# Block numbers for TensorE: 32 loaded at the head of a turn instead of 16 at every second group, in all passes of a graph network kernel

## The reference

```python
# block 0, per layer: weighted mean of the neighbours
msg = h[src] * edge_weight[:, None]
h = h @ W_self.T + segment_sum(msg, dst) * inv_deg @ W_neigh.T + b
# block 1: attributes of the edges
m = (h * norm_out)[src] * (a_mu + exp(a_ls) * edge_attr)
h = segment_sum(m, dst) * norm_in @ W + b
# block 2 (GATv2, 5 heads): attention over pairs
e = leaky_relu(xl[src] + xr[dst]); alpha = einsum(e, att)
out = segment_sum(softmax_by_dst(alpha) * xl[src], dst)
# block 3 (RGAT, 8 relations, 4 heads): scores by edge type
alpha = leaky_relu(q[etype, dst] + k[etype, src])
out = segment_sum(softmax_by_dst(alpha) * xw[etype, src], dst)
```

## Time and profile before

| what | value |
|---|---|
| time, median of 3 runs | 9910.92 us (9910.38 to 9911.04) |
| span of the profiled execution | 11974.2 us |
| TensorE matmul busy | 7534.2 us (63%), weight loads 5244.5 us (44%) |
| VectorE busy | 7367.7 us (62%) |
| GpSimd busy | 5383.2 us (45%) |
| ScalarE busy | 2310.3 us (19%) |
| mean granted TensorE clock | 0.733 |

### The profile page before, as it was taken

One profiled execution on the slowest core, in us unless ns is written; L12 is line 12 of the kernel. 1 busy time (PEld: TensorE's weight loads), 2 busy tenths in 40 slices (PEclk: granted clock), 3 DMA queues, 4 the chain that ended last, 5 costly groups with the idle time before them and its releaser, 6 DMA issues. The chain is left out here.

```text
span 11974.2 us, 162471 instructions
## 1 busy us (share of the span) xinstructions
PE 7534.2 (63%) x38295; PEld 5244.5 (44%) x38296; DVE 7367.7 (62%) x10447; ACT 2310.3 (19%) x8712; POOL 5383.2 (45%) x5649
## 2 busy tenths in 40 slices
PE   2878788667677775555548555554855554855557
PEld 1666566555555552333347323333732222622226
DVE  6665433355555555677799567778955555745558
ACT  0222344300000001111159111114910000000000
POOL 2555555455545543665400266550015553055550
PEclk9888888788878885777755577775557666867768
DMA  2333344344444444766649566664933333333333
GB/s 60 87 84 84 99 114 114 90 113 111 110 95 113 111 96 163 234 233 231 194 203 411 179 232 232 229 216 173 415 120 74 74 73 63 116 72 75 75 72 100
DMA packets 851293, 1717.47 MB, mean 143 GB/s; under 512 B 384638, under 2 KB 473541, under 8 KB 796922
## 3 DMA queue, kind: packets, MB, share of 16 engines
q1 hardware_dynamic: 465500, 1137.96, 27.5%
q0 software_dynamic: 207456, 413.40, 15.8%
q10 hardware_dynamic: 178256, 165.14, 4.1%
HBM read 1263.59 MB, written 453.99 MB: 143 GB/s over the span
## 5 line engine op out<-in xcount | busy, mean ns | idle before, releaser
L556 POOL DMA_INDIRECT gathered_rows<-node_table,index x2496 | 2379.1, 953 | 2000.0 <-issue 652.4
L719 PE MATMUL ps_G<-table_parts,low_onehots 125*128 125x320 bf16 x15600 | 2712.0, 336 | 294.1 <-issue 220.8
L576 PE MATMUL ps_sum<-messages,onehots 128*125 128x65 f32 (+3 forms) x13312 | 2113.4, 321 | 993.1 <-issue 643.6
L576 PEld LDWEIGHTS ps_sum<-messages,onehots 128*125 128x125 f32 x13312 | 2011.7, 236 | 1117.9 <-issue 1111.2
L556 POOL DMA_INDIRECT gathered_rows<-xl_table,index x1664 | 1576.7, 948 | 1828.5 <-issue 1028.0
L556 POOL DMA_INDIRECT gathered_rows<-rel_table,index x1456 | 1391.9, 956 | 2009.8 <-ACT index L546 1020.9
L1524 PE MATMUL ps_Z<-xr,onehots_wide 125*128 x3328 | 1505.3, 610 | 1194.5 <-issue 628.4
L719 PEld LDWEIGHTS ps_G<-table_parts,low_onehots 125*128 125x128 bf16 x15600 | 1677.7, 110 | 1183.2 <-issue 312.8
L749 DVE TENSOR_TENSOR rows_by_feature<-ps_G,fifth_onehots 128x320 f32<-128x320 f32 x1040 | 507.0, 487 | 2271.9 <-remote 1683.0
L1524 PEld LDWEIGHTS ps_Z<-xr,onehots_wide 125*128 125x128 f32 x3328 | 801.4, 257 | 1899.3 <-issue 1802.7
L1572 DVE TENSOR_TENSOR z<-gathered_rows,ps_Z 128x650 f32<-128x650 f32 x832 | 670.9, 828 | 835.4 <-issue 499.7
(11 more groups left out here) (326 smaller groups left out, 7209.2 us busy)
## 6 DMA issues: line engine op xcount, KB each, us to landing
stash_a<-gathered_rows SPq DMA_DIRECT2D x208, 1300.0 KB
kept_rows<-stash_a SPq DMA_DIRECT2D x208, 1300.0 KB
onehots<-onehots_kept SPq DMA_DIRECT2D x520, 500.0 KB
onehots_turned<-onehots_turned SPq DMA_DIRECT2D x416, 250.0 KB
stash_r<-gathered_rows ACTq DMA_DIRECT2D x208, 272.0 KB
kept_rows<-stash_r SPq DMA_DIRECT2D x208, 272.0 KB
low_rows<-low_rows SPq DMA_DIRECT2D x416, 125.0 KB
onehots_kept<-onehots ACTq DMA_DIRECT2D x104, 500.0 KB
```

The costliest lines, as they stand in the source:

```text
L556: pool.indirect_dma_start(G[:, HALF * k + q, 0:width], None, table, bass.IndirectOffsetOnAxis(IDX[:, k, q:q + 1], 0)).then_inc(gathered[k] ...
L576: return nc.tensor.matmul(ps_sum[0:BN, bass.ds(at, width)], S[:, j, :], M, start=False, stop=True, skip_group_check=True)
L719: last = nc.tensor.matmul(ps_G[:, (fetch * k + g) % 2, 0:D * FIVE], OT[0:BN, k, g, a, :], HP[:, part, a, :, :].rearrange("p f b -> p (f b) ...
```

## The change

In all six places the load is made at group 0 alone, for all 32 chunks of the turn, and the indexing loses its `% PAIR`. The number of block numbers loaded per turn stays 32, the number of load instructions goes from two to one per turn. The three forms of the edit:

```diff
-                                if k % 2 == 0:
-                                    at = blocks_of(i * U + HALF * k, PAIR)
+                                if k == 0:
+                                    at = blocks_of(i * U, U)
...
-                                    last = sum_chunk(ps_sum, S, j, M[:, j, :], D, at[j % PAIR] * D)
+                                    last = sum_chunk(ps_sum, S, j, M[:, j, :], D, at[j] * D)
```

```diff
-                                if m % 8 == 0:
-                                    at = blocks_of(i * U + 2 * m, PAIR)
+                                if m == 0:
+                                    at = blocks_of(i * U, U)
```

```diff
-                                    if q == 0 and h % 2 == 0:
-                                        at = blocks_of(HALF * (HT * i + h), PAIR)
+                                    if q == 0 and h == 0:
+                                        at = blocks_of(HALF * HT * i, HALF * HT)
```

More of the change, by code:

```diff
@@ L35 @@
 GROUPS = NCH // HALF
-PAIR = 2 * HALF
 NG = NS // HALF
@@ L903, in turn @@
                                 n = K * i + k
-                                if k % 2 == 0:
-                                    at = blocks_of(i * U + HALF * k, PAIR, places[0:1, :], (NB - 1) * (D + 1) + (NB - 1) // PER * (BANK - PER * (D + 1)))
+                                if k == 0:
+                                    at = blocks_of(i * U, U, places[0:1, :], (NB - 1) * (D + 1) + (NB - 1) // PER * (BANK - PER * (D + 1)))
                                 if not hist:
@@ L922, in turn @@
                                 for j in range(HALF * k, HALF * (k + 1)):
-                                    last = sum_chunk(ps_sum, S, j, M[:, j, :], D + 1, at[j % PAIR])
+                                    last = sum_chunk(ps_sum, S, j, M[:, j, :], D + 1, at[j])
                                 last.then_inc(chunk_done.sem, HALF)
@@ L1524, in _ @@
                                     last = nc.tensor.matmul(ps_Z[:, m % 2, q, 0:PW], SW[0:BN, j % WIDE, :],
-                                                            XR[:, bass.ds(at[j % PAIR] * PW, PW)], start=True, stop=True)
+                                                            XR[:, bass.ds(at[j] * PW, PW)], start=True, stop=True)
                                 last.then_inc(dest_made.sem, 1)
@@ L1705, in turn @@
                                     last = nc.tensor.matmul(ps_Q[:, q // QH, q % QH * QW:(q % QH + 1) * QW], ST[0:BN, j, :],
-                                                            XQ[:, bass.ds(at[j % PAIR] * QW, QW)], start=True, stop=True)
+                                                            XQ[:, bass.ds(at[j] * QW, QW)], start=True, stop=True)
                                 last.then_inc(dest_made.sem, 1)
@@ L1961, in _ @@
                                         pe.wait_ge(own_copied.sem, own_copied.at(HT * i + h + 1))
-                                    sum_chunk(ps_sum, S, j, M[:, j, :], out_w, at[j % PAIR] * P).then_inc(chunk_done.sem, 1)
+                                    sum_chunk(ps_sum, S, j, M[:, j, :], out_w, at[j] * P).then_inc(chunk_done.sem, 1)
                         nc.tensor.matmul(ps_sum[:, 6 * BANK + 3 * P:7 * BANK], zero[:, 0:P], zero[:, 0:P], start=False, stop=True,
```

## The result

| | before | after |
|---|---|---|
| time, median | 9910.98 us (9910.38 to 9911.29, 4 runs) | 10179.95 us (10178.14 to 10182.01, 4 runs) |
| ratio, with its 95% interval | 1 | 1.0271 (1.0257 to 1.0286) |

The change costs 269 us. The forecast was 9900 us with a range from 9862 to 9940: wrong in sign and far outside.

The account below looks back on a forecast made before the run. It took POOL's gathers to bound eight passes and TensorE's sequencer passes 10 and 12. Only those two gained, 0.21 x 26 x 2 = 11 us, all others 0: 9911 - 11 = 9900 us, range 9862 to 9940.

Parts of the forecast that it names:

- The price of a load: TensorE's sequencer, L527: a load of 32 numbers goes by the number and takes 2.17 us; two of 16 take 2.21.
- Rival A: Loads on L527: one round trip whatever the count, 1.11 us; passes 10 and 12 gain 47 us, 9864 us; chance 0.13.
- What the timed run is: Whole kernel: the trace without the odd stretches, eight passes bound by POOL's gathers, passes 6, 8, 10, 12 as traced.
- Rival C: Loads on L527: 32 numbers load as two of 16, only the register step goes; 6 us, 9905 us; chance 0.07.
- Rival B: Passes 1, 3, 4: TensorE sets the timed turn, 1.06 us longer each; 83 us less 11, 9983 us; chance 0.20.
- Passes 1 to 4: Gathering passes: TensorE's path grows 1.06 us a turn at the head, hidden by POOL's 30.0 us; effect 0.
- Passes 6 and 8: Passes waiting for messages: a load 1.06 us longer still ends before the messages come; effect 0, turn 18.0 us in 6.
- Passes 10 and 12: Only TensorE's sequencer is full there; it gains what its work shrinks, 0.21 us a turn, 11 us in all.
- two dispatch terms: Parts of the sequencer's 0.21 us a turn: dispatch of the register step (within 0.12) and of the second load (0.05).
- The prediction's own sign: Whole kernel: a time above 9930 us would mean that TensorE's path carries the timed turns too.
- The cover: TensorE's work queued behind a load: 17 matmuls or about 2.0 us, less than a load of 2.17.
- The chances: Whole kernel's time: faster 0.18, same (within 0.2%) 0.62, slower 0.20.

Follow-up runs that it names:

- e2: Kernel before with the change in the ten passes other than 10 and 12: 9904.46 us against 9903.97, ratio 1.0001.
- e0: Kernel before, unchanged, profiled once more for a trace without the odd stretch: 9899.76 us, median of before 9903.97.
- e8: Kernel before with one wait a group (for messages) instead of three in passes 10 and 12: 11780.54 us against 11815.57, ratio 0.9968.
- e5: Kernel before with four loads of 8, one at each group, in passes 10 and 12: 10148.48 us against 9899.47.
- e14: The same kernel as e8, with more runs on another chip: 11893.53 us against before's 11934.51, ratio 0.9968.
- e13: Kernel before with four loads of 8 and one wait a group in passes 10 and 12: 11876.98 us against 11934.51, one run.
- e12: Kernel before with, in passes 10 and 12, one load of 32, one wait a group and two zero matmuls ahead of the load: 11926.72 us, ratio 1.000.
- e6: Kernel before with the change in passes 10 and 12 only, plus four small zero matmuls ahead of the load: 9929.55 us against 9899.47.
- e10: Kernel before with one more wait step a group in passes 10 and 12, loads unchanged: 12079.80 us against 11815.57, one run.
- e4: Kernel before with loads of 24 at the head and 8 at group 3 in passes 10 and 12: 10161.25 us against 9899.47.
- e9: The whole change in all passes, plus one wait a group instead of three in passes 10 and 12: 12080.46 us against before's 11815.57, ratio 1.0223.
- e1: Kernel before with the change in passes 10 and 12 only: 10163.85 us against 9903.97.
- e3: Kernel before with both loads of 16 behind each other at the head of the turn in passes 10 and 12: 10168.38 us against 9903.97.
- e11: Kernel before with the change in passes 10 and 12 only, plus four small zero matmuls at group 2: 12036.52 us against 11815.57.
- e7: Kernel before with the change in passes 10 and 12 only, plus one 512-column zero matmul at group 2: 10107.77 us against 9899.47.

## Why the prediction was wrong

Step by step, by its own headings.

**The price of a load: right.** 2.13 us measured, 2.17 taken from ScalarE's rows. Rival A, the single round trip, is refuted by the four sizes: 0.59, 1.107, 1.62 and 2.13 us for 8, 16, 24 and 32 numbers, 64 ns a number.

**What the timed run is: right.** Rival C fell with the count of loads (312). The eight passes with gathers go at POOL's 30.0, 40.0 and 35.0 us a turn, and the trace of after shows them without the odd stretch. Rival B needed TensorE to set the turns of passes 1, 3 and 4; e2 shows ten passes with the change at 1.0001.

**Passes 1 to 4: right, stall and all.** The longer load did go straight onto TensorE's path there. The idle behind it is 0.7 and 0.8 us in the median turn of passes 3 and 4 in e0, and 1.8 us in both in after: about the 1.06 us more that were forecast, on an idle larger than the 0.26 of the earlier trace rows. The clock falls there too. The fetch behind the idles of this turn of pass 3 takes 7.09 us instead of 4.24, at a mean granted clock of 0.59:

```profile
2003.56 1.95 PE L575 MATMUL ps_sum<-messages,onehots 128*125 128x64 f32 x16 [2.48 <-DVE messages L1024]
2007.34 7.09 PE L718 MATMUL ps_G<-table_parts,low_onehots 125*128 125x320 bf16 x30 [1.82 <-issue]
2014.27 1.86 PE L575 MATMUL ps_sum<-messages,onehots 128*125 128x64 f32 x16
2015.96 4.24 PE L718 MATMUL ps_G<-table_parts,low_onehots 125*128 125x320 bf16 x30
```

But it comes back by the end of that one fetch (1.00 from 2014.5 on), and POOL's 30 us hide all of it. e0 has such slow fetches too (6.59 us at 2020.81), so this is not new with the change.

**Passes 6 and 8: right**, 18.0 and 17.8 us in e0 and in after.

**Passes 10 and 12: the step that failed.** "A sequencer that never rests gains what its work shrinks: 0.21 x 26 x 2 = 11 us." The premise holds (e8: the sequencer binds, and eight waits fewer give 0.75 us a turn). The conclusion leaves TensorE itself out. The prediction wrote "what changes is where it stalls: 1.06 us longer at the head", priced that in passes 1 to 4, where POOL hid it, and never in passes 10 and 12, because there only the sequencer's sum seemed to count. But the stall decides how long TensorE idles at one place: 0.95 us in after, where e0 has 0.29 at the same head and 0.51 to 0.58 at all later ones. Behind that idle the granted clock fell from 1.00 to 0.50, and a turn became 64 x 0.210 = 13.4 us of array, 5.3 us more than before. From then on the array set the turn, and 0.21 us less work for the sequencer was worth nothing. Whether the 0.21 would have come at the upper clock no run shows, since after has only its first turn there. No run shows its two dispatch terms apart either (half of the 0.12, and the 0.05): they were the author's estimate. What e5 shows in their place: with two loads and two steps more its third turn took 8.57 us where before's take 8.10, of which the loads themselves are 4 x 0.59 - 2 x 1.107 = 0.15, so 0.16 for a step and both dispatches together, against 0.12 + 0.05. The prediction's own sign, that a time above 9930 us would mean TensorE's path in the gathering passes, points to the wrong passes.

**The cover: half right.** The prediction saw about 2.0 us of sums queued ahead of a load, too little for one of 2.17; that is why it expected a longer idle. Its rows show 2.0 us only for the second load of the turn; at the first, which starts at 3116.0, the sums end at 3117.2, so 1.2 us were queued. In pass 10 it was 1.6 us in after and 1.03 in before, so the stall of 1.03 us more was met by 0.57 us more of cover, and 0.43 us were left.

**The chances.** Every case priced a microsecond of stall as a microsecond. Rival B, the only slower case, had 0.20 and at most 9983 us. A clock that falls and stays turns 0.43 us more of idle into 5.3 us a turn, which none of the cases contained. The earlier trace rows had shown a fetch at 6.59 us instead of 4.25 behind a stall (granted clock 0.63 against 1.00), and rival B named the lower clock, but only as a way for TensorE to become the bound of passes 1, 3 and 4. The same row should have made a rival for passes 10 and 12, where TensorE has little time to spare: 7.0 us of matmuls in a turn of 8.1.

What makes the clock fall, in the runs of passes 10 and 12:

| kernels | idle of TensorE in a turn, us | clock |
|---|---|---|
| e8, e14 | up to 0.19 | kept |
| e13 | 0.27 to 0.33 | kept |
| e12 | 0.35 to 0.42 | kept |
| e6 | 0.50 to 0.56, with wider matmuls ahead | kept |
| before, e0 | 0.51 to 0.58 and 0.14 to 0.20 | kept |
| e5 | 0.52 and three of 0.08 | fell, in the fourth turn of pass 10, in the third of pass 12 |
| e10 | 0.68 to 0.82 and 0.39 to 0.45 | fell, in the third turn of pass 10, in the fourth of pass 12 |
| e4, e9 | 0.73 to 0.81 | fell behind the first |
| after, e1, e3 | 0.95 to 1.20 | fell behind the first |

Two things are shown: a longer idle in a stream of narrow sums makes it fall (e1, e3, e4 against e0), and zeros that fill the idle keep it (e6), while the same zeros elsewhere don't (e11). What is not settled is how the chip weighs the idle. The longest idle alone does not sort the runs: e5's is before's, and e5 fell. The length of the turn for the same 7.0 us of matmuls does not either: before's is 8.1 us, e5's and e10's are 8.6 and fell, e13 has e5's loads in 7.8 us and kept its clock, but e9 fell behind a first turn of 7.9. Both seem to count. Whether the width of the matmuls in between counts as well no run here separates. In e7 and e11 the clock went up and down, with turns between 9.0 and 14.9 us; in the changed kernel it went down once and stayed.

## What to carry to other kernels

Before merging two short stalls of TensorE's sequencer into one long one, ask what idle of TensorE it makes, and look at the granted clock in that stage: the sum of the stalls is not the cost, because an idle of 0.95 us in a stream of narrow matmuls cost 5.3 us in every turn after it (after, granted clock 0.50). A loop that just keeps the clock was fragile here: four wait steps a turn, 26 us of work, cost 264 us (e10). Where such a loop is bound by its sequencer, take work from the sequencer (waits that another wait implies) rather than move its stalls; where the stall must stay, a few zero matmuls queued ahead of it kept the clock here (1.00 in e6, 0.99 in e12).

## What the runs showed of the hardware that I had not expected

- The lower clock stayed in the narrow sums. In after TensorE is busy in every part of 280 us with sums of 68 columns and stays at 0.50. Before's sums are the same and stay at 1.00 with two idles a turn. With wider zero matmuls between the sums it came back for a time (0.86 and then 1.00 behind the wide one in e7, 0.84 and then 1.00 behind the four in e11); in passes 10 and 12 of the kernels that fell the narrow sums never did.
- A load that does not matter can be much longer: in passes 5 and 7 of after the loads of 32 take 4.5 to 4.7 us in the median, up to 5.07, against 2.13 elsewhere, and the turn stays at 40 us. It is not the change: in e0 the loads of 16 take 3.7 us there in the median, against 1.107. What makes them longer was not tried.
- The odd stretch of some 10 us a turn that the prediction ascribed to the profiled execution is in the timed runs of two series: before took 9904, 9899, 11816 and 11935 us in the four, the second and the fourth on the same chip. The trace of e8, of an execution of 11777.56 us, shows it: in pass 3 the sums that start at 3122.61 give way to the next fetch only at 3135.01. What brings it is not known. The effect of the change in passes 10 and 12 was the same on them: e9, which has e8's waits besides, lost 265 us where before takes 11816, the change 269 where it takes 9911.
